# Attention over edges: the matmuls of the destinations set between two unit sums, one-hot tiles widened earlier, encoders two groups ahead

## The reference

```python
h = (x @ W.T).reshape(n, H, D)                      # H = 8 heads, D = 32
alpha = sum(h[src] * a_src) + sum(h[dst] * a_dst)   # one score for each edge and head
enc = relu(edge_attr @ edge_W.T + edge_b).reshape(-1, H, D)
alpha = alpha + sum(enc * h[dst])
alpha = where(alpha >= 0, alpha, 0.2 * alpha)
ex = exp(alpha - segment_max(alpha, dst)[dst])
attn = ex / segment_sum(ex, dst)[dst]
out = segment_sum(h[src] * attn, dst) + bias
```

## Time and profile before

| | |
|---|---|
| median of 3 runs | 2460.91 us (2457.75 to 2461.18) |
| profiled execution, its own time | 2461.9 us |
| its span in the trace | 2460.1 us |
| attention, by its first and last instruction | from 1409.1 to 2112.4 us of the span |
| busy over the span: TensorE, VectorE, GpSimd, ScalarE | 73%, 63%, 43%, 36% |

### The profile page before, as it was taken

How to read it: one execution, slowest core, us unless ns; L and a number is a source line. 1 busy time by engine, 2 the same in 40 slices (tenths; PEclk the granted TensorE clock), 3 DMA queues, 4 the chain that set the end, 5 groups by cost and what they waited for, 6 DMA issues and landing times. The chain is left out here.

```text
span 2460.1 us, 41170 instructions
## 1 busy us (share of the span) xinstructions
PE 1795.0 (73%) x11452; PEld 1396.4 (57%) x11452; DVE 1538.4 (63%) x3157; ACT 893.4 (36%) x2297; POOL 1066.1 (43%) x1106
## 2 busy tenths in 40 slices
PE   3366666655099987499973777777778787499598
PEld 1255445444077766499962556666666664255587
DVE  7655555654187767665548467777777775464443
ACT  7433333332000002333323645555555554244221
POOL 0377777777600000155530077666666660000243
PEclk9678888888599999599996989999999997599799
DMA  3355554544398851522224155555454550533353
GB/s 85 115 190 191 196 184 172 180 167 173 118 327 291 291 196 54 189 72 71 72 84 150 56 168 160 153 147 145 145 147 140 145 147 26 191 124 115 125 179 104
DMA packets 203756, 368.02 MB, mean 150 GB/s; under 512 B 63193, under 2 KB 111162, under 8 KB 203159
## 3 DMA queue, kind: packets, MB, share of 16 engines
q1 hardware_dynamic: 148066, 205.99, 25.4%
q0 software_dynamic: 54624, 159.35, 20.6%
q10 hardware_dynamic: 850, 0.04, 0.0%
HBM read 235.32 MB, written 130.87 MB: 149 GB/s over the span
## 5 line engine op out<-in xcount | busy, mean ns | idle before, releaser
L2137 POOL DMA_INDIRECT att_rows<-hdram,top_ix x440 | 419.6, 954 | 337.3 <-POOLq L1579 132.4
L2221 PE MATMUL att_p_sum<-att_msg,att_hot 128*128 128x264 f32 x880 | 272.7, 438 | 59.4 <-ACT att_hot L2273 49.5
L874 POOL DMA_INDIRECT mtab<-first_w,msgs_ix x280 | 274.7, 981 | 85.3 <-issue 80.2
L1177 POOL IOTA route_spare<- 128x65 f32 (+1 forms) x2 | 0.4, 177 | 573.2 <-POOLq L1115 573.2
L2221 PEld LDWEIGHTS att_p_sum<-att_msg,att_hot 128*128 128x128 f32 x880 | 175.3, 211 | 124.1 <-issue 70.4
L736 PE MATMUL msgs_p_m<-nodes_n,msgs_hott 128*128 x592 | 184.9, 467 | 47.7 <-issue 28.4
L874 POOL DMA_INDIRECT mtab<-msgs_rw,msgs_ix x160 | 159.5, 997 | 68.9 <-issue 45.4
L637 DVE TENSOR_TENSOR first_w<-msgs_p_m,msgs_sorted 128x1024 f32<-128x1024 f32 x70 | 85.6, 1223 | 143.2 <-PE msgs_p_m L736 119.2
L2337 DVE TENSOR_TENSOR att_enc<-att_enc,att_p_h 128x1024 f32<-128x1024 f32 x110 | 134.2, 1220 | 64.8 <-PE att_p_h L2167 64.8
L736 PEld LDWEIGHTS msgs_p_m<-nodes_n,msgs_hott 128*128 128x128 f32 x592 | 132.0, 235 | 75.0 <-issue 54.5
L2167 PE MATMUL att_p_h<-heads_parts,att_hz 128*128 x1320 | 173.7, 285 | 0.8 <-DVE att_enc L2337 0.8
(11 more groups left out here) (402 smaller groups left out, 3819.4 us busy)
## 6 DMA issues: line engine op xcount, KB each, us to landing
first_w<-mtab SPq DMA_DIRECT2D x77, 520.0 KB, 4.6
etab<-msgs_et SPq DMA_DIRECT2D x110, 288.0 KB, 2.5
att_hz<-etab SPq DMA_DIRECT2D x110, 288.0 KB, 3.0
msgs_rw<-mtab SPq DMA_DIRECT2D x45, 520.0 KB, 4.6
htab<-hid_hr SPq DMA_DIRECT2D x12, 1024.0 KB, 4.3
first_w<-in_L_ffn_w SPq DMA_DIRECT2D x16, 512.0 KB, 5.0
ffn0x_w<-in_L_ffn_w SPq DMA_DIRECT2D x16, 512.0 KB
ffn_w<-in_L_ffn_Wd SPq DMA_DIRECT2D x8, 1024.0 KB
```

What stands on the lines that cost most here:

```text
L874: nc.gpsimd.indirect_dma_start(mtab, bass.IndirectOffsetOnAxis(ap=ix[:, g, q:q + 1], axis=0), rw[g % RS][:, q, :], None).then_inc(s_free[g ...
L2137: nc.gpsimd.indirect_dma_start(rows[:, g % RS, q, :], None, hdram, bass.IndirectOffsetOnAxis(ap=ix1[:, g, q:q + 1], axis=0)).then_inc(s_ro ...
L2221: last = T.matmul(p_sum, hot[g % 2][:, q, :], msg[g % 2][:, q, :], start=(u == 0 and r == 0), stop=(u == NU - 1 and r == UQ - 1), skip_gro ...
```

## The change

On TensorE the order in a step becomes: first unit sum, register loads for the next group, `line` or `tops`, `destinations`, second unit sum, `offsets`, `encoders`, then `turn_back` or `edge_tops`. The encoders run two groups ahead, not one. On ScalarE `weights` and `widen` come between the two copies of the bank, and `encodings`, two groups ahead, behind the second copy. `enc` gets a third buffer, `hz` an eleventh, and the two buffers `hot` now lie in memory of weights of an earlier stage.

```diff
-    RS, SE = 12, 10
+    RS, SE = 12, 11
-    hot = [a.sb(f"hot{s}", [P, G, P]) for s in two]
+    hot = [lent.rearrange("p (q d) -> p q d", q=G) for lent in spare]
-    enc = [a.sb(f"enc{s}", [P, G, C]) for s in two]
+    enc = [a.sb(f"enc{s}", [P, G, C]) for s in range(3)]
...
             destinations(0)
+            encoders(1)
             for s in range(NUG + LAG + 1):
                 if 0 <= at < NU:
                     sums(at)
+                if s + 1 < NUG:
+                    own_tiles(s + 1)
                 if j == 0 and 0 < t <= NB:
                     line(t - 1)
                 if j == 1 and 0 < t <= NB:
                     tops(t - 1)
+                if s + 1 < NUG:
+                    destinations(s + 1)
+                if 0 <= at < NU:
+                    sums(at + 1)
                 if s < NUG:
                     offsets(s)
-                if s + 1 < NUG:
-                    own_tiles(s + 1)
-                    encoders(s + 1)
-                if 0 <= at < NU:
-                    sums(at + 1)
-                if s + 1 < NUG:
-                    destinations(s + 1)
+                if s + 2 < NUG:
+                    encoders(s + 2)
...
             encodings(0)
-            widen(0)
+            encodings(1)
...
-                if s + 1 < NUG:
-                    encodings(s + 1)
+                if 0 <= s - LAG < NUG:
+                    weights(s - LAG)
+                    widen(s - LAG)
                 if 0 <= at < NU:
                     keep_totals(at + 1)
+                if s + 2 < NUG:
+                    encodings(s + 2)
                 if j == 0 and 0 < t <= NB:
                     copy_back(t - 1)
                 if j == 1 and 0 < t <= NB:
                     falls(t - 1)
-                if 0 <= s - LAG < NUG:
-                    weights(s - LAG)
-                if 0 < s - LAG < NUG:
-                    widen(s - LAG)
```

More of the change, by code:

```diff
@@ L2064, in split, with attention @@
     link(V.tensor_copy(parts[2], rest))
-def attention(nc, a, cst, etab, segtab, ewz, ix1, penn, gb, keep, hparts, hdram, acc):
-    RS, SE = 12, 10
+def attention(nc, a, cst, etab, segtab, ewz, ix1, penn, gb, keep, hparts, hdram, acc, spare):
+    RS, SE = 12, 11
     two = range(2)
@@ L2255, in encodings @@
                 act.wait_ge(s_z, g + 1)
-                if g >= 2:
-                    act.wait_ge(s_red, g - 1)
-                S.activation(enc[g % 2][:], p_z[:], ACT.Relu).then_inc(s_enc, 1)
+                if g >= 3:
+                    act.wait_ge(s_red, g - 2)
+                S.activation(enc[g % 3][:], p_z[:], ACT.Relu).then_inc(s_enc, 1)
             def weights(g):
@@ L2333, in products @@
             def products(g):
-                t, j, e = g // BG, g % BG, enc[g % 2]
+                t, j, e = g // BG, g % BG, enc[g % 3]
                 dve.wait_ge(s_h, g + 1)
@@ L2487, in build @@
                 with ExitStack() as c1:
-                    attention(nc, Pool_(nc, c1, "att"), cst, etab, segtab, ewz, ix1, penn, gb[1], buckets[1], hparts, hdram, acc)
+                    attention(nc, Pool_(nc, c1, "att"), cst, etab, segtab, ewz, ix1, penn, gb[1], buckets[1], hparts, hdram, acc,
+                              [wts["wn"][:].rearrange("p k c -> p (k c)"), wts["gabe"][:].rearrange("p r c -> p (r c)")])
             reuse_semaphores(nc)
```

## The result

| | before | after |
|---|---|---|
| median | 2461.05 us (2457.75 to 2461.72) | 2389.84 us (2387.42 to 2394.84) |
| ratio, 95% interval | | 0.9716 (0.9697 to 0.9735) |
| profiled execution, its own time | 2461.9 us | 2394.84 us |
| its span | 2460.1 us | 2393.1 us |
| first copy of the bank to the copy 101 steps later | 603.7 us | 539.1 us |

Between the two profiled executions the difference is 67.0 us of span, and it divides so: the attention's first copy comes 3.2 us later (stages ahead of it, with unchanged code), the loop gives 64.6, the last nine steps 2.7, and what follows 2.9. Nearly all of it is in the loop, where the forecast had it too.

A forecast was written before the change was run, and what follows sets the result against it. No engine is full; the order of handovers bounds the kernel. Blocks 1.65 us shorter, times 25.25, give 42 us, the last steps 4: 46 us off 2461.9 is 2416, against the median 2415 us; range 2390 to 2460 us.

The forecast's parts named there:

- signs that the prediction named: Destinations some 1.45 us behind a first sum, no wait for `widen`, step 0 near 5.1 us, clock over 0.98, step 3's waits.
- Destinations at 1.45 us: On TensorE, with register loads ahead, `destinations` start 1.45 us behind the first sum; ends given as 0.89 and 1.97 us.
- Both rivals on the loads: Loads begin after an empty array: destinations at 1.97 us, 2492 us, chance 0.09; loads hold nothing up: 0.9 us, 0.05.
- the third rival: Register loads hold nothing up in TensorE's list: destinations at 0.9 us, 20.6 us a block, 2373 us; chance 0.05.
- Steps 0, 2 and 3: Steps of a block of four in the loop: 5.07 us (was 6.11), 5.27 us, and 5.9 us (was 4.96).
- The new wait of step 3: VectorE's `alphas` wait for offsets behind the second sum, then TensorE's next sum for `lessen`: 5.9 us, was 4.96.
- Step 1: The step with `tops`, which move destinations to 2.23 us; TensorE's list sets its 6.03 us, was 6.2 or 7.7.
- The clock: TensorE's clock stays up in the loop, saving about 30 us; rival that it falls as before: 2445 us, chance 0.13.
- the fourth rival: The order gives back what it takes, through late links in the chain of a block's scores: about 2458 us; chance 0.11.
- Cover that was costed at nothing: The encoders' relu beside the next first sum, `copy_back` behind it, table loads, and GpSimd's ring freed by `messages`: no cost.
- The last nine steps: Steps without destinations, at 1.2 GHz: `widen` leaves the path, 0.84 us in five or six steps, 4 us.
- The case in which they keep the full clock: Low end of the forecast: 0.97 us less in each of some 16 sums of the last steps, 15 us.

## Why the prediction was right, and where its size was off

**What bounds the kernel.** Right: with no engine full, the order of handovers decides, and taking one wait off the path (`widen`) moved the time by 75 us, with no instruction added or taken away. All the signs that the prediction named came.

**Destinations at 1.45 us.** Measured 1.44 and 1.46 in steps 3 and 0. Both rivals on the loads fall: neither 1.97 nor 0.9 us came. That the loads hold something up is shown by moving them, 26 us; the time then, 2363.70 us, is near the 2373 us that the third rival gave for loads that hold nothing up. The rule in the Trainium skill, "Advanced Engine Details and Errata", section "Sequencer Loop", that engine instructions can be queued while a control instruction is executed, is not borne out for these loads. That `destinations` start 0.3 to 0.4 us earlier without them does not speak against it, since they use the loaded registers; but `line` does not, and starts at 0.96 us without the loads and at 1.30 us with them. `copy_back`, which the prediction costed at nothing, is not what holds `tops`: in the step 1 shown it ends at 1761.08 (1760.81 + 0.27), 0.39 us before they start, and 0.36 to 0.53 us before in all 25 blocks.

**Steps 0, 2 and 3.** Forecast 5.07, 5.27 and 5.90, measured 5.05, 5.10 and 5.71. `destinations` take 1.30 to 1.37 us until the next instruction, not 1.40, and in step 2 they start at 1.58 on average (1.45 to 1.63), not 1.7. The new wait of step 3 is there as it was written, in each of 25 blocks.

**Step 1 is the term that was mis-sized.** Forecast 6.03, measured 5.34, which is 0.69 of the 1.07 us by which the block was wrong (22.27 against 21.20 by the means). Three pieces make it, all in the timeline of step 1 above:
- `tops` were to move `destinations` by 0.78 us, to 2.23. They start at 1.76 us (1760.12 to 1761.88), 0.31 later than without `tops`. The 0.78 was read from a step in which the loads stood behind the 16 matmuls and the clock was about to fall; in the step of the earlier trace rows it is already less, as its encoders show, 2.91 - 2.25 = 0.66:
```profile
1606.01 0.59 PE L2158 MATMUL att_p_z<-top_ewz,att_hz 128*128 128x512 bf16 x2 [1.10 <-issue]
```
  In the kernel after the loads come first, and `tops`, which then start at 1.35 us, hold the array for 0.41 us, no more.
- `destinations` took 1.30 us, not 1.40.
- TensorE's list after the second sum was to take 2.40 us, a sum of durations from other steps. It took 0.90 + 0.30 + 0.43 + 0.64 = 2.27 us (1763.18 to 1765.45), hardly more than the 2.17 of the chain.

Together 0.47 + 0.10 + 0.13 = 0.70 us a block, 17.5 us in 25 blocks; steps 0, 2 and 3 have another 0.37 us a block, 9.3 us. Of these 27 us some are lost again: the first step of the stretch, in which the clock falls, takes 8.9 us against 7.0 before, and the attention's first copy comes 3.2 us later.

**The clock.** Right: 1.00 in the loop, and the price of about 30 us was close to the 25 that the run with added matmuls showed. The reason was incomplete. The prediction hung it on lulls that the whole rebuilt block no longer has; the move of `widen` alone is enough, and so are the rest of the change without that move, and added matmuls in two places. With `widen` moved, the idle 1.04 us ahead of the first sum of a step 1 are gone. They can't be the whole reason: in the run without that move TensorE is idle up to 1.2 us ahead of its first sums, and the clock stays at 1.00. What keeps it up in each of these kernels stays open. In the kernel before, 19 of 25 steps 1 took 7.5 to 8.6 us and six took 6.2 to 6.35; why the clock fell in some blocks and not in others, no run told.

**Which edit brings the gain.** Here the working said too little. It priced the four steps as a whole, and never the one-hots alone. By the runs, that move has the whole gain: alone it gives 75 us, the rest alone 26, and both 71. The 25 us of the clock are in either and can be won only once, and beyond them the rest gives next to nothing. The matmuls' new order moves the loads' hold from the second sum (2.67 us behind the first before, 2.8 after) to `destinations`, adds the wait of step 3, and so gives back what it takes: against the run with `widen` moved alone, step 1 is 0.79 us shorter, step 3 is 0.75 us longer, and steps 0 and 2 are 0.17 and 0.11 us longer. That is the outcome of the fourth rival for this one move, though by another way: not by late links of the chain of scores, but by the second sum and the offsets of step 3. It is worth 13 us only when the loads are moved away.

**Cover that was costed at nothing.** GpSimd: right, it waits 12 us for messages, its gathers run almost without a break, and what needs their rows waits for them once. The early encoders: they are no addition at no cost, as the prediction had them, but a condition; without them the same kernel is 80 us slower.

**The last nine steps.** 2.7 us against 4. The case in which they keep the full clock did not come, and its size, some 15 us, was right: 14.2 us when added matmuls hold the clock.

Open is why 16 small matmuls moved the encoders of before by 0.66 us and `destinations` of after by 0.31. What was shown is both numbers, not the difference in issue behind them.

## What to carry to other kernels

When a change makes several moves, price each by itself from the rows before the whole: here one move off the path had all the gain, and another paid for itself only with a third. A duration that was read in one place in an engine's list (16 small matmuls ahead of register loads) isn't the duration in another place; bound it from both sides by the array's time and the issue time. And put register loads where their engine waits anyway.

## What the hardware showed that was not expected

- Added matmuls that nothing reads made the kernel faster, twice: 25 us in a loop whose clock fell now and then (granted clock 0.94 to 1.00), and 14 us in the last nine steps, which ran at 1.2 GHz from about the second on (0.50 to 1.00). A unit sum takes 1.13 us at one clock and 2.10 us at the other, and the sums here are on the path.
- Two register loads behind a sum hold what stands behind them in TensorE's list, even matmuls that use none of the registers: `line` starts 1.30 us after the start of the sum with the loads between, and 0.96 us without them. Moving the loads was worth 26 us, against 65 us for the whole loop's gain.
